# An attention and feed-forward kernel: the last stage's products in split halves, its scaling and adding on other engines, and a deeper order of steps

## The reference

```python
query = h @ Wq.T                                     # 64 wide
router_scores = (query @ Wr.T) . (aux_keys @ Wr.T) / sqrt(48) + log_rel   # 256 slots
top_scores, top_idx = top_k(router_scores, 8)
attn = query . aux_keys[top_idx] / sqrt(64) + log_rel[top_idx]
w = softmax(attn)                                    # over the 8
aux_out = (w @ aux_values[top_idx]) @ Wvd.T @ Wvu.T
u = clip(0.5*log1p(var(h))/mean(log1p(var(h))) + 2.5*sigmoid(learned(h)), 0, 5)
gate = sigmoid(gate_w1*clip((u-0.5)/1.5, 0, 1) + gate_bias), 0 where under 0.05
x = x + h + gate * aux_out
```

## Time and profile before

| | |
|---|---|
| Time, median of 3 runs | 716.09 us (713.03 to 716.78) |
| Time of the profiled execution | 715.13 us |
| Its span in the trace | 713.3 us |
| Mean granted TensorE clock | 0.986 of full speed |
| Busy, share of the span: PE, PEld, DVE, ACT, POOL | 91%, 77%, 85%, 52%, 45% |
| Last product of the hidden stage ends | 644.38 us |

### The profile page before, as it was taken

How to read it: one execution, slowest core, us unless ns; L and a number is a source line. 1 busy time by engine, 2 the same in 40 slices (tenths; PEclk the granted TensorE clock), 3 DMA queues, 4 the chain that set the end, 5 groups by cost and what they waited for, 6 DMA issues and landing times.

```text
span 713.3 us, 11497 instructions
## 1 busy us (share of the span) xinstructions
PE 645.7 (91%) x3974; PEld 546.0 (77%) x3974; DVE 604.6 (85%) x858; ACT 369.5 (52%) x522; POOL 323.1 (45%) x233
## 2 busy tenths in 40 slices
PE   3688999999999999999999999999898897997996
PEld 2576878878787878888787878788787897994443
DVE  3589998999989999999999999989968444756996
ACT  2345655555564646565465645555537354554332
POOL 2224345555473545565564645455452826640000
PEclk9899999999999999999999999999999899999999
DMA  8334353343434343434434343442341000000343
GB/s 310 99 93 114 103 162 105 107 119 94 127 101 118 101 128 101 129 113 118 119 100 124 100 122 108 125 114 69 91 125 54 0 1 1 1 1 1 159 161 153
DMA packets 52765, 72.56 MB, mean 102 GB/s; under 512 B 10146, under 2 KB 43492, under 8 KB 52452
## 3 DMA queue, kind: packets, MB, share of 16 engines
q1 hardware_dynamic: 52708, 71.83, 33.6%
HBM read 29.85 MB, written 8.39 MB: 54 GB/s over the span
## 4 chain that ended last, share of the span: by engine, by line
PE 59%; DVE 22%; issue 9%; SPq 4%; DMA 2%; POOL 2%; ACT 1%; DVEq 0%; ACTq 0%
PE gm L438 14%; PE ob L461 8%; DVE qm L953 5%; PE turn L422 5%; SPq L337 4%; PE gm L511 3%; PE turn L511 3%; DVE nkm L923 3%; PE q_slot L398 3%; PE q_slot L396 3%; PE q_slot L397 3%; DVE qsum L963 3%; DVE x_all L976 3%; DVE st L983 2%; PE k_slot L396 2%
## 5 line engine op out<-in xcount | busy, mean ns | idle before, releaser
L845 POOL TENSOR_TENSOR qs_sb<-qs_sb,qrec 128x1024 f32<-128x1024 f32 x64 | 122.2, 1909 | 242.8 <-DVE qrec L967 242.8
L438 PE MATMUL gm<-ekT,ctxT 128*128 128x256 f32 x512 | 121.0, 385 | 25.1 <-DVE mt_sb L944 21.4
L673 ACT ACTIVATE ek<-k_slot,nkm 128x1024 f32<-128x1024 f32 x64 | 71.5, 1117 | 133.4 <-DVE nkm L923 133.4
L438 PEld LDWEIGHTS gm<-ekT,ctxT 128*128 128x128 f32 x512 | 96.6, 191 | 45.6 <-issue 26.9
L461 PE MATMUL ob<-mt_sb,q_hd 128*128 128x128 f32 x1024 | 126.7, 277 | 2.7 <-ACT o_sb L694 2.6
L461 PEld LDWEIGHTS ob<-mt_sb,q_hd 128*128 128x128 f32 x1024 | 121.9, 192 | 8.3 <-issue 5.7
L683 ACT ACTIVATE qs_sb<-qs_sb 128x1024 f32<-128x1024 f32 x64 | 67.9, 1061 | 71.0 <-DVE qs_sb L956 71.0
L953 DVE TENSOR_REDUCE qm<-q_slot 128x16 f32<-128x1024 f32 x64 | 76.5, 1196 | 28.0 <-PE q_slot L398 28.0
L923 DVE TENSOR_REDUCE nkm<-k_slot 128x1 f32<-128x1024 f32 x64 | 76.0, 1187 | 6.1 <-PE k_slot L398 6.1
L928 DVE STREAM_TRANSPOSE kt<-ek 128x1024 f32<-128x1024 f32 x64 | 79.0, 1235 | 2.1 <-ACT ek L673 2.1
L956 DVE TENSOR_TENSOR qs_sb<-q_slot,qm 128x1024 f32<-128x1024 f32 x64 | 78.4, 1225 | 2.2
(11 more groups left out here) (160 smaller groups left out, 1188.3 us busy)
## 6 DMA issues: line engine op xcount, KB each, us to landing
ekT<-kt SPq DMA_DIRECT2D x512, 64.0 KB, 2.0
ctx_in<-ctx_rows SPq DMA_DIRECT2D x16, 512.0 KB, 4.5
x_all<-x SPq DMA_DIRECT2D x16, 512.0 KB, 3.6
ctxT<-ctx_cols SPq DMA_DIRECT2D x16, 512.0 KB, 4.0
out<-q_hd SPq DMA_DIRECT2D x16, 512.0 KB, 2.6
Wuq_in<-Wuq_cols SPq DMA_DIRECT2D x1, 1280.0 KB, 5.3
x_all<-values_cols SPq DMA_DIRECT2D x1, 1024.0 KB, 7.2
WvuT<-WvuT_raw SPq DMA_DIRECT2D x1, 512.0 KB, 4.6
```

The source lines that it names most:

```text
L438: last = nc.tensor.matmul(gm[:, cols], ctxT[:, b % 2, j, :], ekT[:, 2 * half:2 * half + 2, :, j * BLK:(j + 1) * BLK], start=(j == 0), stop ...
L845: nc.gpsimd.tensor_tensor(e, e, qrec[:, i % 2, :].unsqueeze(2).broadcast_to([P, PAIR, DH]), ALU.mult).then_inc(q_mul, 1)
```

## The change

- **f in fp32r.** `WvuT` is loaded twice over, in partitions 0 to 63 and 64 to 127 (`WvuT_in`), and split into `WvuT_hi` (ScalarE copy) and `WvuT_lo` (GpSimd subtraction). `VV` holds its 64 columns twice, so z comes out twice. `zT` is rounded to fp32r, and VectorE replaces its lower half by the remainder (`z_low`, new). f is then four fp32r products of 512 columns, two with each of the halves, in place of two fp32 ones.
- **The output.** ScalarE scales f by `oscale` into `y_out` (`f_scale`, new), and GpSimd adds `X` in place, for b = 0 to 13. For the last two VectorE does both as before, in two halves of 512 columns that are stored one by one. `y_out` has four slots. The reciprocal and the scale are made for two sequences at a time.
- **The mask.** `tensor_scalar(replaced > NEG, * NEG)` reads only `replaced`; one `tensor_tensor_reduce` adds the logits and makes the maximum (a minimum of the negated sum, so `exp` gets `scale=-1`).
- **The order.** TensorE's step i is score(i), z(i - 2), transposes(i - 1), f(i - 3). Scores 0 and 1 are made in the hidden stage, in the two halves of `k_slot`. The logarithm moves from the end of the hidden stage to its step 10, followed there by the copy that makes `WvuT_hi`; GpSimd makes `WvuT_lo` after `hidden_sum(10)`. The mean moves to steps 12 and 13. The gate's instructions stand in steps 1 and 2 of the value stage.

```diff
@@ TensorE, hidden_step @@
+                if b == EARLY + 5:
+                    pe.wait_ge(logsum_done, 1)
+                    pe.wait_ge(query_done, 2 * (b - EARLY - 1))
+                    nc.tensor.matmul(logtotal_psum, ones[:, :], logsum[:, :], start=True, stop=True).then_inc(logtotal, 1)
...
+                if b == B - 1:
...
+                    for n in range(2):
+                        score(n)
@@ TensorE, value stage @@
             def f_product(b, k):
-                pe.wait_ge(z_copied, b + 1)
-                wait(pe, y_ready, b - 1)
+                pe.wait_ge(z_split, b + 1)
+                if b == 0:
+                    pe.wait_ge(logits_ready, 2)
+                wait(pe, f_scaled, b - 1)
                 for n in range(2):
-                    last = nc.tensor.matmul(slot[k][:, n * HALF:(n + 1) * HALF], zT[:, k, :],
-                                            WvuT[:, n * HALF:(n + 1) * HALF], start=True, stop=True)
+                    cols = slice(n * HALF, (n + 1) * HALF)
+                    nc.tensor.matmul(slot[k][:, cols], zT[:, k, :], WvuT_hi[:, cols], start=True, stop=False)
+                    last = nc.tensor.matmul(slot[k][:, cols], zT[0:VB, k, :], WvuT_lo[:, cols], start=False,
+                                            stop=True)
...
+            for i in range(1, B + 3):
+                if 2 <= i < B:
+                    score(i)
+                if has(i - 2):
+                    z_product(i - 2, i % 2)
+                if has(i - 1):
+                    w_transpose(i - 1, (i - 1) % 2)
+                if has(i - 3):
+                    f_product(i - 3, (i - 3) % 2)
@@ ScalarE @@
-                if b == B:
+                if b == EARLY + 2:
                     act.wait_ge(varh_step, 2)
                     nc.scalar.activation(logv[:, :], varh[:, :], ACT.Ln, bias=ones[:, 0:1]).then_inc(logv_done, 1)
+                    act.wait_ge(wvu_in, 16)
+                    nc.scalar.copy(WvuT_hi[:, :], WvuT_in[:, :]).then_inc(wvu_hi, 1)
...
+            def f_scale(b, k):
+                act.wait_ge(oscale_done, b // 2 + 1)
+                act.wait_ge(f_prod, b + 1)
+                wait(act, out_stored[b % YB], 16 * (b // YB))
+                nc.scalar.mul(y_out[:, b % YB, :], slot[k][:, :], oscale[:, b, :]).then_inc(f_scaled, 1)
+
+            for i in range(1, B + 2 + BY_VECTOR):
+                if has(i - 1):
+                    softmax_exp(i - 1, (i - 1) % 2)
...
+                if 0 <= i - 4 < B - BY_VECTOR:
+                    f_scale(i - 4, i % 2)
+                if has(i - 2):
+                    zT_copy(i - 2, i % 2)
+                if has(i - 1):
+                    wT_copy(i - 1, (i - 1) % 2)
@@ GpSimd @@
             for b in range(EARLY, B):
                 hidden_sum(b)
+                if b == EARLY + 2:
+                    pool.wait_ge(wvu_hi, 1)
+                    nc.gpsimd.tensor_tensor(WvuT_lo[:, :], WvuT_in[0:VB, :], WvuT_hi[0:VB, :].bitcast(F32),
+                                            ALU.subtract).then_inc(wvu_lo, 1)
+
+            for b in range(B - BY_VECTOR):
+                pool.wait_ge(f_scaled, b + 1)
+                pool.wait_ge(y_done, b + 1)
+                nc.gpsimd.tensor_tensor(y_out[:, b % YB, :], y_out[:, b % YB, :], X[:, b, :],
+                                        ALU.add).then_inc(y_ready, 1)
@@ VectorE @@
-                V.tensor_tensor(outside[:, :], replaced[:, :], small[k][:, 0:NSLOT],
-                                ALU.is_equal).then_inc(outside_done, 1)
+                V.tensor_scalar(outside[:, :], replaced[:, :], NEG, NEG, ALU.is_gt, ALU.mult).then_inc(outside_done, 1)
                 dve.wait_ge(outside_done, b + 1)
                 wait(dve, w_done, b - 1)
-                V.scalar_tensor_tensor(logits[:, k, :], outside[:, :], NEG, small[k][:, NSLOT:2 * NSLOT], ALU.mult,
-                                       ALU.add).then_inc(masked, 1)
...
-                V.tensor_reduce(nlmax[:, k:k + 1], logits[:, k, :], AX, ALU.max, negate=True).then_inc(logits_ready, 1)
+                V.tensor_tensor_reduce(logits[:, k, :], score_psum(b)[:, NSLOT:2 * NSLOT], outside[:, :], -1.0, -NEG,
+                                       ALU.add, ALU.min, nlmax[:, k:k + 1]).then_inc(logits_ready, 1)
...
+            for b in range(EARLY, B + 1):
...
+                if b == B:
+                    top(0, 0)
+                hidden_step(b)
+            for i in range(1, B + 2):
+                if i < B:
+                    top(i, i % 2)
...
+                if has(i - 2):
+                    z_low(i - 2, i % 2)
+                if has(i - 2) and i % 2 == 0:
+                    output_scale(i - 2)
+            for b in range(B - BY_VECTOR, B):
+                finish(b, b % 2)
```

More of the change, by code:

```diff
@@ L139, in attention_ffn_kernel @@
         query = sb("query", [P, B, C], scope=ffn)
-        WvuT = sb("WvuT", [P, N], scope=ffn)
+        WvuT_in = sb("WvuT_in", [P, N], scope=ffn)
+        WvuT_hi = sb("WvuT_hi", [P, N], F32R, ffn)
+        WvuT_lo = sb("WvuT_lo", [VB, N], F32R, ffn)
         bu2 = sb("bu2", [P, 1], scope=ffn)
@@ L628, in _ @@
             pe.wait_ge(query_done, B)
[L629 to L647, removed]
+            pe.wait_ge(wvu_hi, 1)
+            pe.wait_ge(wvu_lo, 1)
+            for i in range(1, B + 3):
[7 more added lines that the diff above has]
+                    f_product(i - 3, (i - 3) % 2)
         @block.scalar
@@ L1101, in top, with gate_value @@
+            def gate_value():
+                dve.wait_ge(gate_tanh, 2)
+                V.tensor_scalar(ga[:, :], gb[:, :], 0.5, 0.5, ALU.mult, ALU.add).then_inc(gate_step, 1)
+                dve.wait_ge(gate_step, 4)
+                V.scalar_tensor_tensor(gate[:, :, 0], ga[:, :], EARLY_EXIT, ga[:, :], ALU.is_ge,
+                                       ALU.mult).then_inc(gate_done, 1)
             def top(b, k):
                 dve.wait_ge(scores, b + 1)
-                wait(dve, masked, b)
@@ new lines, in output_scale, with z_low @@
+            def output_scale(b):
+                dve.wait_ge(w_done, b + 2)
+                V.reciprocal(wrec[:, b:b + 2, :], wsum[:, b:b + 2, :]).then_inc(wrec_done, 1)
+                dve.wait_ge(wrec_done, b // 2 + 1)
+                dve.wait_ge(gate_done, 1)
+                V.tensor_tensor(oscale[:, b:b + 2, :], wrec[:, b:b + 2, :], gate[:, b:b + 2, :],
+                                ALU.mult).then_inc(oscale_done, 1)
+            def z_low(b, k):
+                dve.wait_ge(z_copied, b + 1)
+                V.tensor_tensor(zT[VB:P, k, :], z_psum[VB:P, :], zT[VB:P, k, :].bitcast(F32),
+                                ALU.subtract).then_inc(z_split, 1)
@@ L1133, in finish @@
             def finish(b, k):
-                dve.wait_ge(oscale_done, b + 1)
+                dve.wait_ge(oscale_done, b // 2 + 1)
                 dve.wait_ge(f_prod, b + 1)
                 dve.wait_ge(y_done, b + 1)
-                wait(dve, out_stored[k], 16 * (b // 2))
-                V.scalar_tensor_tensor(y_out[:, k, :], slot[k][:, :], oscale[:, :], X[:, b, :], ALU.mult,
-                                       ALU.add).then_inc(y_ready, 1)
-            def value_step(b):
-                if b < B:
-                    top(b, b % 2)
-                if has(b - 2):
-                    output_reciprocal(b - 2)
-                if b < B:
-                    replace(b, b % 2)
-                if has(b - 2):
-                    output_scale(b - 2)
-                if b < B:
-                    mask(b, b % 2)
-                    logit_max(b, b % 2)
-                if has(b - 2):
-                    finish(b - 2, b % 2)
@@ L1182, in _ @@
-            dve.wait_ge(gate_done, 1)
-            for b in range(1, B + 2):
-                value_step(b)
+                wait(dve, out_stored[b % YB], 16 * (b // YB))
+                for half in range(2):
+                    cols = slice(half * HALF, (half + 1) * HALF)
+                    V.scalar_tensor_tensor(y_out[:, b % YB, cols], slot[k][:, cols], oscale[:, b, :], X[:, b, cols],
+                                           ALU.mult, ALU.add).then_inc(y_last, 1)
+            for b in range(EARLY, B + 1):
+                if b == EARLY + 4:
+                    dve.wait_ge(logv_done, 1)
+                    V.reduce_sum(logsum[:, :], logv[:, :], AX).then_inc(logsum_done, 1)
+                if b == EARLY + 5:
+                    log_mean()
+                if b == B:
+                    top(0, 0)
+                hidden_step(b)
```

165 lines of the change are left out of this document (83 added, 82 removed).

## The result

| | before | after |
|---|---|---|
| Time, median of 4 runs each, side by side | 714.56 us (711.92 to 716.78) | 724.64 us (717.67 to 727.44) |
| Time of the profiled execution, its span | 715.13, 713.3 us | 724.76, 722.9 us |
| Mean granted TensorE clock of that execution | 0.986 | 0.971 |
| Busy, share of the span: PE, DVE, ACT, POOL | 91%, 85%, 52%, 45% | 90%, 84%, 53%, 50% |

The changed kernel takes 1.0113 times as long (95%: 1.0071 to 1.0154): slower by some 8 us of 715. The medians themselves lie 10.1 us apart; the ratio is estimated over the runs of both kernels and not from the medians. The forecast was 721 beside the 716.09 shown, 5 us more.

The account below looks back on a forecast made before the run. TensorE's chain, 3.46 us a sequence, bounds the kernel, VectorE nearly as full. Hidden stage +5.9, then 12.9 to the maximum of b = 3, 44.2 for twelve steps, 11.2 to the end: span 718.6, time 721; range 708 to 728.

Parts of the forecast that it names:

- the price of f: Value stage, TensorE: f's four fp32r products of 512 columns take 0.94 us instead of 1.72; other end 0.86.
- the waits that were forecast beside it: Value stage: VectorE's mask and scale wait until GpSimd's running instruction ends, 3.3 us of each pair of steps.
- rival 1: Value stage: VectorE's waits don't arise or stay under 0.85 us a step; twelve steps take 32, time 707 to 708; 20%.
- rival 4: Steady value stage: TensorE's clock falls, as it idles some 2 us each pair; if it stays low, about 740 us; 3%.
- the pair of 7.37: Value stage: two steps repeat with 7.37 us, 3.7 a step against 3.46 before, VectorE working 4.0 of it.
- rival 3: Value stage: reciprocal or maximum blocked as well, waits fill GpSimd's whole time; pair 8.8 us, time up to 730; 9%.
- The gap: Hidden stage: TensorE idles 2.9 us before a transpose of step 12, as GpSimd makes WvuT_lo ahead of hidden_sum(11).
- the mean's wait: Hidden stage, step 13: TensorE waits 0.8 us for VectorE's query copies of step 12, before the mean's product (0.4).
- The 1.8 for the clock: Hidden stage: 1.8 us added for TensorE running at the lower clock after its idle stretch.
- To the maximum of b = 3: From the last hidden product to that maximum: 11.9 us, plus 1.0 for the lower clock.
- The end: From the last maximum to the span's end: 11.2 us, with exp, f_scale, last sum and scale, four half finish, stores.
- The sum: Whole kernel: span 718.6 us against 713.3 before, +5.3; median 721.4, said as 721.

Follow-up runs that it names:

- experiment 10: Kernel before with only the new mask (tensor_scalar and one reduce in place of three instructions): 715.7 us, ratio 1.0001 to the kernel before.
- experiment 7: Changed kernel with only WvuT_lo filling 128 partitions, so all four products of f load 128 rows: 720.7 us, ratio 1.0069 to the kernel before.
- experiment 1: Changed kernel with one operand of both the mask and the scale in PSUM: 716.8 us, ratio 1.0017 to the kernel before.
- experiment 3: Changed kernel with GpSimd's additions of X for b = 0 to 13 left out: 713.6 us, ratio 0.9970 to the kernel before.
- experiment 9: Changed kernel with each GpSimd addition of X cut into four pieces of 256 columns: 716.1 us, ratio 1.0023 to the kernel before.
- experiment 5: Changed kernel with only the mask reading PSUM, the scale keeping two SBUF inputs: 715.9 us, ratio 1.0000 to the kernel before.
- experiment 6: Changed kernel with only the scale's reciprocal kept in PSUM, the mask staying SBUF to SBUF: 721.8 us, ratio 1.0070 to the kernel before.
- experiment 4: Changed kernel with GpSimd making WvuT_lo behind its last hidden sum: 721.1 us, ratio 1.0079 to the kernel before.
- experiment 8: Changed kernel with mask and scale operands in PSUM, WvuT_lo in 128 partitions and made behind the last hidden sum: 707.1 us, ratio 0.9860 to the kernel before.
- experiment 2: Changed kernel with mask and scale operands in PSUM and WvuT_lo in 128 partitions: 710.4 us, ratio 0.9913 to the kernel before.

## Why the prediction was right, and where it was not

The forecast had the direction, the mechanism in the steady steps, and a time within 4 us. That the time came out so near is in part luck: the price of f was wrong by 0.74 us a step, and the waits that were forecast beside it covered the mistake.

- **What bounds it.** TensorE's chain of 3.46 a step set the kernel before: experiment 10 took an instruction from VectorE and won nothing.
- **What becomes cheaper.** Wrong for f: 0.94 was forecast, with 0.86 as the other end, and it took 1.68. The rows used had 128-row loads throughout; the changed f alternates them with 64-row ones. TensorE's step was 3.23, not 2.65. The waits hid this mistake: full rows alone moved the steps by 0.9 us. It also makes rival 1 wrong in its price: without waits the time is 716.8, not 707 to 708. And TensorE idles only 0.45 us in 10, where the forecast had some 2 in each pair; the clock stayed at 1.00 there, so rival 4 did not arise. The other durations held: reduce 0.425 (0.42), mask free 0.29 (0.28), `z_low` 0.295 (0.28), `f_scale` 1.09 to 1.11 (1.12), the addition 2.36 (2.4).
- **What they cost each other.** Right. The pair is 7.15 (forecast 7.37, or 7.1 with a shorter `f_scale`), alternating 5.0 and 2.1 from one maximum to the next. Experiments 1, 3 and 9 show the mechanism, 5 and 6 that the mask's wait is enough to cause the loss. (The forecast's VectorE work of 4.0 a pair is 4.1 by its own terms; the pair of 7.37 stands.) Steps 4 and 5 took 4.69 each, with the mask blocked in both, which the forecast's pairs did not have: 45.4 against 44.2.
- **What does not wait.** The reciprocal took 0.17 us beside GpSimd's additions (681.14), and in experiment 1 the maximum 0.42 inside one (the row below), so neither is among the blocked ones and rival 3 is refuted. The mask took 0.29 from SBUF (experiment 3) and 0.42 from PSUM (experiment 1), and only the former waits. The Trainium skill's table of modes (VectorE: DVE Perf Modes, "The perf-mode tier table") gives fp32 `tensor_scalar` in SBUF the double rate; the trace agrees in kind (0.29 against 0.42). The forecast used it only to say that no wait would change; here the faster form is the one that waits. Another page of the Trainium skill (SBUF — State Buffer, "🔬 SBUF: two separate sides") calls the ports that the two engines share an exclusive lock, held for a whole instruction. The trace agrees in experiment 9.

```profile
679.16 0.42 DVE L1191 CUSTOM_DVE_ANT_0 logits<-ob,outside 128x256 f32<-128x256 f32 x1
```

- **Hidden stage.** The gap was forecast at 2.9 and is 2.90; the mean's wait was forecast at 0.8 and is 0.91, its product at 0.4 and took 0.21. The 1.8 for the clock did not occur in the profiled execution, whose hidden stage took 4.5 more where 5.9 were forecast. A fall of the clock occurred in six of the eight profiled executions with this gap, and cost 1.5 to 2.7.
- **To the maximum of b = 3.** It took 12.1 against 12.9, of which 1.0 was for the clock. TensorE idled 3.65 of the 6 us from 650 on, and the clock fell behind it (0.72 from 656 to 662), as the forecast had it; which other term of the sum was too long stays open.
- **The end.** Mis-sized: 11.2 forecast, 15.4 measured. 12.3 to 12.4 is what it takes at full clock (experiments 1, 4 and 8); the last `finish` ends 8.3 behind the maximum there (experiment 4), and the forecast's terms had it at 7.0. (Its terms add up to 11.1, not 11.2.) The other 3.0 us are the clock, which fell at 708 us and which I had not considered at this place.
- **The sum.** +5.3 on the span was forecast, +9.6 measured, of which 1.25 lie in attention, which the change hardly touches. Mistakes of both signs are in it: hidden stage -1.4, the start -0.8, steps +1.2, the end +4.2.

## What to carry to other kernels

Before giving GpSimd elementwise work beside a VectorE that has little slack, list each VectorE instruction with two SBUF inputs, and each `tensor_scalar` from SBUF to SBUF, however small: each may wait for the rest of GpSimd's instruction. The mask's share came back by letting it read and write PSUM, or by cutting GpSimd's work into pieces, without giving up the move. A cheaper product shows only when the wait that covers it is gone, so price each engine's step as if it were alone (experiment 7 against 2), and take the price of a product from rows with the same weight loads.

## What was not expected of the hardware

- **Weight loads that change their rows.** A load takes about as long either way (in the change 183 ns for 64 rows, 188 for 128 in f). fp32r products of 512 columns were 0.23 apart when each load had 128 rows (experiment 2), 0.43 when loads of 128 and 64 rows alternated, and then each load began only 0.24 us after the one before it had ended. Mixed loads are not the only case of it: in the kernel before, loads of 128 rows for the fp32 products of f (at 666.55 and 666.98) have 0.24 before them as well.
- **The same idle stretch, another clock.** Behind the idle 2.9 us of the hidden stage the next step (transposes to the mean's product) took 5.75 in two executions at clock 1.00, 7.28 in three (experiments 5, 6 and 7) and 8.49 in three others (experiments 1, 2 and 3), where the stretch from 630 to 640 us had 0.66 to 0.71. With 0.92 idle (experiments 4 and 8) it took 5.75 in both. After 1.50 idle at the end the clock fell in the change (to 0.50), but not in experiment 4, where the same row has the same 1.50. This may be a part of the scatter of the change's runs (717.67 to 727.44), which is not shown; which execution gets which clock stays open.
